# Graph layer on one core: node phase with the table ahead of q, k, v, edge tables inside it, seven gather slots

## What is computed

```python
xn = layernorm(x)                                     # 6250 x 256
# graph attention
feat = xn @ W_n                                       # 8 heads x 32
el, er = feat . attn_l, feat . attn_r                 # per node, 8 heads x 4
e = leaky(sum_t((el[src] + er[dst] + e16 @ attn_m) * e4) / 3)
a = segment_softmax(e, dst)
gnn = segment_sum(feat[src] * a, dst)
# linear attention
q, k, v = split(xn @ Wqkv)
q = softmax(q, over the 32 of a head) * SCALE
k = softmax(k, over all nodes)
mix = layernorm_gamma((q @ (k.T @ v)) @ Wout)
x = x + gnn + mix
x = x + moe_ffn(layernorm(x))
```

## Time and profile before

| | us |
|---|---|
| median of 3 runs | 3594.44 (3593.63 to 3603.38) |
| profiled execution, its own time | 3594.56 |
| its span, first to last instruction | 3592.9 |
| TensorE busy | 3076.7 (86%) |
| VectorE busy | 2724.5 (76%) |
| ScalarE busy | 1675.6 (47%) |
| GpSimd busy | 1648.0 (46%) |

### The profile page before, as it was taken

One profiled execution on the slowest core, in us unless ns is written; L12 is line 12 of the kernel. 1 busy time (PEld: TensorE's weight loads), 2 busy tenths in 40 slices (PEclk: granted clock), 3 DMA queues, 4 the chain that ended last, 5 costly groups with the idle time before them and its releaser, 6 DMA issues. The chain is left out here.

```text
span 3592.9 us, 79682 instructions
## 1 busy us (share of the span) xinstructions
PE 3076.7 (86%) x21675; PEld 2485.6 (69%) x21676; DVE 2724.5 (76%) x5311; ACT 1675.6 (47%) x5730; POOL 1648.0 (46%) x1798
## 2 busy tenths in 40 slices
PE   7988617888888888888888888888859999999999
PEld 4666405676776767677666767676638888888888
DVE  4667726888888888888888888888858776777776
ACT  3433203555555555555555555555533333333333
POOL 2210227777777777777777777777500000000000
PEclk9987858999999999999999999999969999999999
DMA  2200336666666666666666666666421000100000
GB/s 77 78 33 18 105 119 181 180 184 178 182 180 184 181 178 182 176 181 176 182 181 181 182 179 183 182 181 181 126 77 57 19 19 20 37 19 20 19 10 13
DMA packets 346109, 434.87 MB, mean 121 GB/s; under 512 B 156833, under 2 KB 254144, under 8 KB 345838
## 3 DMA queue, kind: packets, MB, share of 16 engines
q0 software_dynamic: 85616, 259.65, 26.9%
q1 hardware_dynamic: 260222, 172.47, 16.5%
HBM read 374.16 MB, written 57.73 MB: 120 GB/s over the span
## 5 line engine op out<-in xcount | busy, mean ns | idle before, releaser
L846 POOL DMA_INDIRECT gat<-scratch_table,idx x1616 | 1553.3, 961 | 508.2 <-issue 481.9
L1162 PE MATMUL ps_s<-msg,oh 128*128 128x272 f32 x4000 | 1013.9, 402 | 27.7 <-ACT tmp L888 18.7
L1162 PEld LDWEIGHTS ps_s<-msg,oh 128*128 128x128 f32 x4000 | 734.0, 191 | 165.1 <-ACT tmp L888 24.7
L1014 DVE TENSOR_TENSOR msg<-gat,ps_m 128x2048 f32<-128x2048 f32 x250 | 560.6, 2284 | 91.5 <-issue 91.5
L1418 ACT ACTIVATE h<-ps_h,fsh,fsc 128x512 f32<-128x512 f32 (+1 forms) x416 | 290.8, 750 | 565.0 <-PE ps_h L1603 565.0
L897 ACT ACTIVATE acc<-acc,sc 128x33 f32<-128x33 f32 x2000 | 459.0, 340 | 162.8 <-DVE acc L1005 162.8
L877 ACT CAST oh<-ps_o 128x1024 f32<-128x1024 bf16 x250 | 259.2, 1037 | 397.7 <-PE ps_o L1102 395.1
L1383 POOL DMA_DIRECT2D out<-y x12 | 9.1, 762 | 923.9 <-DVE y L1558 923.9
L888 ACT ACTIVATE tmp<-ps_s,sc 128x33 f32<-128x33 f32 x2000 | 384.4, 304 | 17.2
L1139 PE MATMUL ps_e<-ident,e 128*16 128x128 f32 x1000 | 149.7, 299 | 258.6 <-DVE e L973 258.6
L1458 DVE CAST h_hi<-h 128x1024 fp32r<-128x1024 f32 (+1 forms) x208 | 137.3, 660 | 239.7 <-ACT h L1418 239.5
(11 more groups left out here) (194 smaller groups left out, 5375.9 us busy)
## 6 DMA issues: line engine op xcount, KB each, us to landing
d16r<-scratch_dst SPq DMA_DIRECT2D x250, 256.0 KB
scratch_acc<-acc SPq DMA_DIRECT2D x250, 136.0 KB
gat<-scratch_table,idx POOLq DMA_INDIRECT x1616
a<-in_a SPq DMA_DIRECT2D x250, 64.0 KB
scratch_table<-trow POOLq DMA_DIRECT2D x49, 144.0 KB, 2.0
am<-scratch_acc SPq DMA_DIRECT2D x12, 544.0 KB, 4.1
xin<-in_x SPq DMA_DIRECT2D x49, 128.0 KB, 2.0
xre<-in_x SPq DMA_DIRECT2D x49, 128.0 KB, 2.0
```

Of the source, the lines that this page charges most:

```text
L846: pool.indirect_dma_start(out=gat[:, s, c, :], out_offset=None, in_=scr["table_rows"], in_offset=bass.IndirectOffsetOnAxis(ap=idx[:, g * C ...
L1014: dve.tensor_tensor(m4[:, :, :, 0:DH], gat[:, row_of(at), :, 0:D].rearrange("p a c (h d) -> p (a c) h d", h=H), ps_p.rearrange("p (c j h) ...
L1162: last = pe.matmul(ps_s[j][:, 0:SUMS], oh[:, s, j, c, :], msg[:, 2 * (s % 2) + j, c, :], start=(c == 0), stop=(c == C - 1), skip_group_che ...
```

## The change

- `GSLOTS` goes from 6 to 7, with the constants that compute a group's slot.
- `tiles` can run a function between the fifth step and the loop (`between`), and can be unrolled throughout (`unrolled`), which TensorE's node loops now are.
- The node phase has four pipelines in place of three. The first makes only the table row; the transposed tile is kept for all tiles in `xq`, and er is kept in f32 (`er_f`). The second multiplies the kept transposes by the q, k, v weights, keeps k and v, writes q over the transpose, updates the maximum of k and does q's exponentials and sums. The third is the context; q is multiplied by its reciprocal sums in it, in place. A column of ones (zero for rows beyond the last node) stands at the end of each tile of v, so that the sum of k comes out of the same matmul. er is split for all tiles at once in five instructions, placed between the steps of the serial part. The fourth is the output.
- The loads of the edge tables are issued after x tile 1, the VectorE work stands after the fifth step of the first pipeline, and the stores follow the last load of x and three weight loads that have moved there. Tables share memory with `ktile`, so ScalarE waits for the fifteen stores before it copies k, q and v. `phase_edge_tables` is gone.
- The store of `xmix` moves from GpSimd to SP, behind the reload of x.

```diff
-GSLOTS = 6
+GSLOTS = 7
@@ def tiles
-def tiles(eng, *stages):
+def tiles(eng, *stages, between=None, unrolled=False):
...
+    if between:
+        between()
+    if unrolled:
+        for t in range(5, NT):
+            step(t, t % 2)
+    else:
...
@@ sync
+                if isinstance(t, int) and t == 1:
+                    for dst, name in ((d_em, "dst_em"), (dn_em, "dst_next_em"), (d_lin, "dst_lin"),
+                                      (dp_lin, "dst_prev_lin")):
+                        sp.dma_start(dst[:, :], io[name].rearrange("(p n) -> p n", p=P)).then_inc(dst_in, 16)
...
             tiles(sp, (load_x, 0))
+            for dst, src in late:
+                sp.dma_start(dst, src).then_inc(late_in, 16)
+            sp.wait_ge(derived, 1)
...
+            for k in range(VK):
+                for name, src in (("visit_group", gt_i[:, 0, k:k + 1]), ...
+                    sp.dma_start(scr[name][k * P:(k + 1) * P].rearrange("(p a) -> p a", a=1), src).then_inc(stored, 16)
...
+            tiles(sp, (reload, 0), (store_mix, 2))
@@ scalar
+            tiles(act, (spread, 0), (turn, 1), (keep_row, 2))
+            act.wait_ge(stored, 16 * STORED)
...
+            def keep(t, s):
+                act.wait_ge(qkv, t + 1)
+                act.copy(flat(ktile, t), ps_qk[s][:, D:2 * D]).then_inc(kept, 1)
+                act.copy(flat(xq, t), ps_qk[s][:, 0:D]).then_inc(kept, 1)
+                act.copy(vtile[:, row_of(t), 0:D]..., ps_v[s][:, 0:D]).then_inc(kept, 1)
+            tiles(act, (keep, 0), (exp_q, 1))
+            tiles(act, (exp_k, 0))
@@ vector
+            tiles(dve, (measure, 0), (norm, 1), between=edge_tables)
+            tiles(dve, (maxima, 0), (sum_q, 2))
...
+            tiles(dve, (shift, 0), (soften, 1))
...
-            tiles(dve, (soften, 0), (finish, 3), (measure_out, 2))
+            tiles(dve, (finish, 1), (measure_out, 0))
@@ tensor
-            tiles(pe, (turn, 0), (project, 1))
+            tiles(pe, (turn, 0), (project, 1), unrolled=True)
+            tiles(pe, (project_qkv, 0), unrolled=True)
...
                 for c in range(KD):
-                    pe.matmul(ps_ft[c][:, 0:D], kexp[:, s, c * P:c * P + P],
-                              vtile[:, row_of(t), :]..., start=start, stop=stop, skip_group_check=True)
-                for c in range(KD):
-                    last = pe.matmul(ps_ft[c][:, D:D + 1], kexp[:, s, c * P:c * P + P],
-                                     real[:, row_of(t)], start=False, stop=stop, skip_group_check=True)
+                    last = pe.matmul(ps_ft[c][:, 0:D + 1], kexp[:, s, c * P:c * P + P], flat(vtile, t),
+                                     start=start, stop=stop, skip_group_check=True)
@@ build
-    phase_edge_tables(nc, io, scr)
```

More of the change, by code:

```diff
@@ L98, in tiles @@
         step(t, t % 2)
-    with eng.Fori(0, (NT - 5) // 2) as k:
-        for u in (0, 1):
-            step(k * 2 + (5 + u), (5 + u) % 2)
+    if between:
[4 more added lines that the diff above has]
+    else:
+        with eng.Fori(0, (NT - 5) // 2) as k:
+            for u in (0, 1):
+                step(k * 2 + (5 + u), (5 + u) % 2)
     for t in range(NT, NT + max(lag for _, lag in stages)):
@@ L241, in reload, with store_mix @@
                     .then_inc(xre_in[s], 16)
-            tiles(sp, (reload, 0))
+            def store_mix(t, s):
+                sp.wait_ge(mixf_ok, t + 1)
+                sp.dma_start(scr["xmix"][row_of(t), :, :].rearrange("a p n -> (a p) n"),
+                             mixf[:, s, :]).then_inc(mix_out[s], 16)
+            tiles(sp, (reload, 0), (store_mix, 2))
+            sp.wait_ge(stored, 16 * (STORED + 1))
+            sp.wait_ge(mix_out[0], 16 * ((NT + 1) // 2))
+            sp.wait_ge(mix_out[1], 16 * (NT // 2))
         @block.gpsimd
@@ L279, in _ @@
[L279 to L283, removed]
         @block.scalar
@@ L296, in turn, with keep_row @@
             def turn(t, s):
[L298 to L303, removed]
+                act.wait_ge(turn_ps, t + 1)
+                settle(act)
+                act.copy(flat(xq, t), ps_tr[s][:, :, :].rearrange("p k n -> p (k n)")).then_inc(turn_ok, 1)
+            def keep_row(t, s):
                 act.wait_ge(proj, t + 1)
@@ L305, in keep @@
                 if later(t):
[L307 to L312, removed]
-                         ps_qk[s][:, D:2 * D]).then_inc(kept, 1)
@@ L314, in keep @@
-                act.copy(vtile[:, row_of(t), :].rearrange("p a n -> p (a n)"),
-                         ps_v[s][:, 0:D]).then_inc(kept, 1)
-            tiles(act, (spread, 0), (turn, 1), (keep, 2))
-            def exp_kq(t, s):
+                    act.wait_ge(table_out[s], (t - s) * 8)
+                act.copy(trow[:, s, :], ps_ft[s][:, 0:ROW]).then_inc(trow_ok, 1)
+                act.copy(flat(er_f, t), ps_ft[s][:, ROW:ROW + HT]).then_inc(trow_ok, 1)
+            tiles(act, (spread, 0), (turn, 1), (keep_row, 2))
@@ L475, in turn, with part @@
                 if later(t):
-                    pe.wait_ge(xnT_ok, t - 1)
+                    pe.wait_ge(turn_ok, t - 1)
                 for k in range(KD):
                     last = pe.transpose(ps_tr[s][:, k, :], xn[:, s, k * P:k * P + P], ident[:, :])
-                last.then_inc(xnT_ps, 1)
+                last.then_inc(turn_ps, 1)
+            def part(t, at, k):
+                return t[:, row_of(at), k * P:k * P + P].rearrange("p a n -> p (a n)")
             def project(t, s):
-                pe.wait_ge(xnT_ok, t + 1)
+                pe.wait_ge(turn_ok, t + 1)
+                if later(t):
+                    pe.wait_ge(trow_ok, (t - 1) * 2)
+                settle(pe)
+                for k in range(KD):
+                    last = pe.matmul(ps_ft[s][:, 0:D + 2 * HT], part(xq, t, k), wcat[:, k, :],
+                                     start=(k == 0), stop=(k == KD - 1))
+                last.then_inc(proj, 1)
@@ L489, in project @@
                 for k in range(KD):
-                    pe.matmul(ps_qk[s][:, :], xnT[:, s, k, :], wqkv[:, k, 0:2 * D],
-                              start=(k == 0), stop=(k == KD - 1))
-                for k in range(KD):
-                    last = pe.matmul(ps_v[s][:, 0:D], xnT[:, s, k, :], wqkv[:, k, 2 * D:3 * D],
+                    last = pe.matmul(ps_v[s][:, 0:D], part(xq, t, k), wqkv[:, k, 2 * D:3 * D],
                                      start=(k == 0), stop=(k == KD - 1))
-                last.then_inc(proj, 1)
@@ L658, in phase_edges @@
+            tiles(pe, (turn_q, 0), (attend, 1), unrolled=True)
 def phase_edges(nc, io, scr):
```

437 lines of the change are left out of this document (198 added, 239 removed).

## The result

The changed kernel takes 3610.24 us (median of 6 runs), the kernel before 3594.95 us beside it: a ratio of 1.0041, 95% interval 1.0027 to 1.0055. It is slower by some 15 us, a little beyond the 0.3% that the prediction gave as the limit of what can be told. The forecast of 3598 was 12 us low.

The account below looks back on a forecast made before the run. TensorE was taken to pace the projections, and chains the context and output stages. Terms of +118, -42, -20 and -52 us moved the edge phase's start from 516.0 to 519.7, +3.7 us, giving 3598 us, range 3568 to 3624.

Parts of the forecast that it names:

- The forecast case: Whole kernel: 3598 us, +3.7 us, not distinguishable from no difference; own range 3588 to 3608, chance 0.42.
- slower rivals: Context loop at half clock (3620 us, chance 0.17) and longer x chain in the first loop (3612 us, chance 0.12).
- table loop, 43 tiles: First loop, paced by two x buffers: 3.28 us per tile, bounds 3.23 and 3.60, 141.0 us in all.
- tile 48 to first k copy: Between the first loops: ScalarE waits 21.8 us after SP's last store issue, copies begin at 208.6 instead of about 190.
- q, k, v and the maximum: Second loop: TensorE at 2.58 us per tile, then the maximum over partitions 6.7 us, ending at 341.7.
- longer x chain: Rival in the first loop: pitch 3.6 us, +14 us, 3612 us; chance 0.12.
- four signs of being right: x measures 3.2 to 3.3 us apart, k copy over 20 us late, q, k, v pitch 2.58, edge phase near 516.
- belongs to the end of a phase: Rival on the wait between loops: the 21.8 us aren't the stores', sum 18.5 us lower, 3580 us; chance 0.16.
- The prediction's sentence on the Trainium skill: Wait between loops: the trace's 21.8 us disagrees with the skill's fixed DMA cost of about 2.0 us.
- half clock: Rival in the context loop: TensorE at the lower clock, 1.75 instead of 1.3 us per tile, +22, 3620 us; chance 0.17.
- straight loops: Rival: context at 1.18 and output at 1.74 us per tile, 17.3 us less, 3581 us; chance 0.13.
- reload and store both leave SP within 1.1 us: Output loop: x reload and output store land 2 us later, under the 4 us after which a buffer is wanted.

Follow-up runs that it names:

- x2_xbuf4: Changed kernel with four x buffers in the first loop instead of two: 3533.79 us, ratio 0.9844.
- x3_spread: Changed kernel with the fifteen table stores and three late weight loads issued singly beside the x loads of tiles 8 to 25: 3618.05 us, ratio 1.0071.
- the two pairs of other rows: Visit tables as 32 rows of 32 bytes, run twice each: in the changed kernel ratios 1.0004 and 1.0004, in the kernel before 0.9983 and 0.9955.
- y3_x4_rows: Changed kernel with four x buffers, 32-row visit tables and an extra iota behind the maximum over partitions: ratio 0.9871.
- z3_er: Changed kernel with four x buffers, 32-row visit tables, extra iota, late weights beside x loads, er split and stored in the q, k, v loop: ratio 0.9825.
- x4_iota: Changed kernel with one more one-column iota on GpSimd right behind the maximum over partitions: 3606.91 us, ratio 1.0043.
- x1_slots6: Changed kernel with six gather slots again instead of seven: 3616.41 us, ratio 1.0069.
- w1_er: The kernel of z3_er run once more for its time, with an edge phase of usual length: 3500.52 us, ratio 0.9738.
- y2_before_rows: Kernel before with visit tables stored as 32 rows of 32 bytes, nothing else changed: ratio 0.9983, edge phase from 494.09 us.

## Why the prediction was right, and where it was off

The forecast case, no difference to be told, had 0.42, slower 0.29. The time fell just beyond its own range (3588 to 3608), inside the whole one (3568 to 3624) and on the side of the slower rivals: +15 us for +3.7. The sum, step by step, against the trace of the changed kernel:

| Step | forecast | measured | difference |
|---|---|---|---|
| tile 5 measured | 39.4 | 38.19 | -1.2 |
| table loop, 43 tiles | 141.0 | 154.7 | +13.7 |
| tile 48 to first k copy | 28.2 | 29.7 | +1.5 |
| q, k, v and the maximum | 133.1 | 129.8 | -3.3 |
| context, transition, to first output | 77.2 | 72.7 | -4.5 |
| first output to edge phase | 100.8 | 105.4 | +4.6 |
| start of edge phase | 519.7 | 530.57 | +10.9 |

The step differences have both signs and partly cancel: 19.8 us too low, 9.0 too high. So the start of the edge phase is met to 11 us in part by luck, and the case that came is not the forecast one but the rival "longer x chain" (3612 us, chance 0.12). Of the four signs of being right only the pitch of 2.58 us in the q, k, v loop appeared; the x pitch (3.60 for 3.2 to 3.3, though VectorE did wait for the load), the first k copy (16.8 us after the last issue for over 20) and the start of the edge phase (530.57 for within 10 of 516) missed.

**First loop.** The mechanism was right (x2_xbuf4 removes it by itself), the size wasn't: the pitch was 3.60, the upper bound, not 3.28. The value was taken from two tiles of the earlier trace rows in the unrolled prologue; in the loop VectorE waited 2.3 us for the load on average (97.2 us in 42 waits) instead of 2.0, most turns were 3.4 to 3.65 and three were over 4. I called the wait of the loop the pace and didn't ask what two more buffers would be worth: 76 us, five times what the whole change costs.

**The wait between the loops.** Its size was forecast well (16.8 us after the last issue, and SP's issues stretched from 5.2 to 10.8 us, together 29.7 against 28.2). That both parts were wrong and their sum right is no chance: counted from the first visit store the stores take 27 us in either kernel. The cause wasn't forecast. The step said that the wait for the stores costs 21.8 us; the rivals were "belongs to the stores" and "belongs to the end of a phase". x3_spread and the two pairs of other rows show a third: it is the shape of these stores, many rows of 4 bytes, and it is paid by whatever is queued at the time, the table rows of GpSimd's queue too. The stores were in the case all along and took 2.7 us each in the earlier trace rows; a DMA share of 0.01 beside a 21.8 us wait hid it. The prediction's sentence on the Trainium skill sets a figure for DMAs that GpSimd issues against stores of SP.

**Second loop and maximum.** TensorE's pitch of 2.58 holds (copies of the last two tiles at 345.44 and 348.01). The maximum was costed at 6.7 from the 8.16 of the earlier trace rows and was 3.3: the reduction began 0.3 us after VectorE's last maximum (349.49 after 349.22) and ended before VectorE was done with the sums of q at 352.3, so nothing waited for it. The 8.16 us had another part than GpSimd's last stores: in the kernel before VectorE's last maximum was over at 217.05, but GpSimd stood for 5.53 us between its last store and the reduction, waiting for nothing that the profile shows:

```profile
224.09 1.08 POOL L271 PARTITION_ALL_REDUCE kmaxb<-kmax  x1 [5.53 <-issue]
```

In the changed kernel GpSimd had been idle for 131.06 us by then, and no such time is seen. That its cost was paid in this idle time isn't tested.

**Context.** 61.7 us for 49 tiles (352.5 to 414.2), 1.26 each instead of 1.3 and 2 to fill, at a clock of 0.95: the rival "half clock" didn't come, and "straight loops" (1.18) came a third of the way.

**Output.** The pitch was 1.96 ((527.88 - 433.81) / 48) against 2.0. What failed is the sentence that reload and store both leave SP within 1.1 us: it counted the queue in the loop and not what stood ahead of it, er's store. Its 6.06 us are in no term of the sum. From the end of the context loop to the first output it was 11.0 us, 11.5 forecast; of this the split of er takes 2.1 rather than 1.2 (11.1 us with it in y3_x4_rows, 8.9 without it in z3_er), and the rest less.

**Edge phase.** Taken as unchanged. The first message came 59.0 us after the phase's start instead of 52.8, almost all of it GpSimd's iota; first to last message then took 5.1 us less than before. The first was shown by x4_iota. The second can't be put down to the slots: with six it was 2038.2 (x1_slots6) and 2040.8 us (before), with seven 2035.7, 2038.5 (x4_iota), 2039.1 (w1_er) and 2039.8 (x2_xbuf4). A step that the prediction moved, the edge tables' two iotas to the front of the kernel, had taken this stall in the kernel before, beside loads that were waited for anyway: that cover was not named.

## What to carry to other kernels

When a change takes the full engine out of a loop, the chain that is next sets the pace at once: count buffers times round trip for the load before counting engines, and deepen the ring in the same edit. A wait behind stores is to be read with the shape of the stores: moving many rows of a few bytes moves their cost onto the next queue, another layout removes it. For each step that is moved ask what else it covered where it stood.

## What the runs showed of the hardware

- From the first of ten stores of 128 rows of 4 bytes to the end of the wait for them it took 27 us in the kernel before, with a DMA share of 0.01 in the last 22 us; with five of 32 rows of 32 bytes it took 3.7 us (y2_before_rows). With the 4-byte stores under way a load of 128 KB took up to 8.2 us instead of 2.1 (x3_spread), and a table store of GpSimd's queue held ScalarE for 14.80 us (changed kernel).
- The first iota after a maximum over partitions waited 6.90 to 9.43 us on GpSimd in the eleven traces with the changed node phase, with nothing shown ahead of it; the next one didn't wait. A memset in between didn't wait either (530.82 in the changed kernel).
- TensorE's granted clock went from 0.65 (40 to 190 us, busy 101.16 of 150) to 0.99 (40 to 105 us, busy 58.72 of 65) in the same loop when only the loads got earlier (x2_xbuf4). The matmuls of a table row took 2.34 us in 31 of 49 tiles of the changed kernel and 1.24 us in 43 of 49 in x2_xbuf4.
